# A graph network's edge stage: TensorE's and ScalarE's operations of one step in another order

## What is computed

```python
m_input  = concatenate([x[src], x[dst], edge_attr], axis=-1)   # 100000 x 320
h        = relu(m_input @ W1 + b1)                             # 100000 x 128
messages = relu(h @ W2 + b2)
agg      = segment_sum(messages, dst)                          # 3125 x 128
updated  = x + relu(agg @ Wn + bn)
```

## Time and profile before

| | |
|---|---|
| median of the runs | 1943.5 us |
| profiled execution, its own time | 1940.99 us |
| its span, first to last instruction | 1939.0 us |
| TensorE busy, share of the span | 1594.3 us, 82% |
| GpSimd busy | 767.6 us, 40% |
| VectorE busy | 731.2 us, 38% |
| ScalarE busy | 692.8 us, 36% |
| mean granted TensorE clock | 0.967 |

### The profile page before, as it was taken

The page is one execution under the profiler, slowest core; times in us unless marked ns, Lnnn a source line. Parts: engine busy times, 40 slices in busy tenths (PEclk is TensorE's granted clock), DMA queues, the critical chain, the costliest instruction groups (busy, mean ns, idle before and its releaser), DMA issues.

```text
span 1939.0 us, 35472 instructions
## 1 busy us (share of the span) xinstructions
PE 1594.3 (82%) x10363; PEld 1041.1 (54%) x10364; DVE 731.2 (38%) x2702; ACT 692.8 (36%) x1413; POOL 767.6 (40%) x805
## 2 busy tenths in 40 slices
PE   2777777998996888888888888888888884994995
PEld 1444445544555666666666666666666663442444
DVE  7998893112233222222222222222222225365004
ACT  4666663002002443444444444444444445301001
POOL 3000000000003777777777777777777761000000
PEclk9999997999997999999999999999999996997998
DMA  1000000001005333333333333333333321000001
GB/s 54 0 0 0 0 0 3 1 1 38 0 1 141 88 80 82 81 81 81 82 81 80 82 82 80 81 81 81 82 81 82 80 67 38 5 1 2 1 0 34
DMA packets 158346, 93.71 MB, mean 48 GB/s; under 512 B 120529, under 2 KB 143824, under 8 KB 158296
## 3 DMA queue, kind: packets, MB, share of 16 engines
q0 software_dynamic: 25088, 51.43, 10.2%
q1 hardware_dynamic: 133208, 41.60, 8.8%
HBM read 86.44 MB, written 6.52 MB: 48 GB/s over the span
## 4 chain that ended last, share of the span: by engine, by line
POOL 26%; PE 18%; issue 17%; DMA 3%; DVE 3%; ACT 1%; SPq 1%; POOLq 0%; DVEq 0%; ACTq 0%
POOL arena L607 26%; PE ps L726 8%; PE ps L929 3%; DMA arena<-x_w1a,idx 2%; PE ps L845 1%; PE ps L855 1%; PE ps L838 1%; PE ps L834 1%; DVE arena L1335 1%; PE ps L825 1%; DMA x_w1b<-arena 0%; DVE stats L1325 0%; PE ps L863 0%; PE ps L939 0%; PE ps L960 0%
## 5 line engine op out<-in xcount | busy, mean ns | idle before, releaser
L607 POOL DMA_INDIRECT arena<-x_w1a,idx x784 | 740.6, 945 | 832.2 <-issue 824.2
L726 PE MATMUL ps<-adj,arena 128*128 (+2 forms) x1875 | 367.7, 358 | 14.6 <-DVE arena L1300 7.9
L726 PEld LDWEIGHTS ps<-adj,arena 128*128 128x128 bf16 x1875 | 172.1, 99 | 203.2 <-issue 26.0
L1473 DVE TENSOR_TENSOR arena<-win_i,drel 128x96 f32<-128x96 f32 x196 | 50.7, 259 | 554.7 <-PE ps L855 551.3
L1117 ACT ACTIVATE arena<-arena 128x512 f32<-128x512 f32 x196 | 123.6, 631 | 302.6 <-DVE arena L1479 302.6
L834 PE MATMUL ps<-ident_f,arena 128*128 128x128 f32 x784 | 126.7, 284 | 126.1 <-DMA arena<-x_w1a,idx 126.1
L845 PE MATMUL ps<-w_c,arena 128*128 128x128 f32 x1568 | 226.9, 288 | 0.0
L660 PE MATMUL ps<-arena 128*128 128x300 bf16 x784 | 164.8, 296 | 63.1 <-DVE arena L1287 63.1
L1113 ACT ACTIVATE arena<-ps,cols 128x512 f32<-128x512 f32 x196 | 134.8, 688 | 218.2 <-PE ps L838 218.2
L845 PEld LDWEIGHTS ps<-w_c,arena 128*128 128x128 f32 x1568 | 189.7, 191 | 40.1 <-issue 40.1
L855 PE MATMUL ps<-arena 128*24 128x128 f32 x1568 | 206.6, 275 | 2.2 <-ACT arena L1117 2.2
(11 more groups left out here) (167 smaller groups left out, 1242.1 us busy)
## 6 DMA issues: line engine op xcount, KB each, us to landing
arena<-in_edge_attr SPq DMA_DIRECT2D x196, 128.0 KB, 2.2
arena<-x_w1a,idx POOLq DMA_INDIRECT x784
arena<-x_w1b SPq DMA_DIRECT2D x196, 12.0 KB
x_spill<-arena SPq DMA_DIRECT2D x1, 1600.0 KB, 7.7
x_w1a<-arena SPq DMA_DIRECT2D x6, 256.0 KB, 2.3
x_w1b<-arena SPq DMA_DIRECT2D x6, 256.0 KB, 2.4
arena<-x_spill SPq DMA_DIRECT2D x6, 256.0 KB, 4.6
out_x<-arena SPq DMA_DIRECT2D x3, 512.0 KB
```

The source lines that it names most:

```text
L607: pool.indirect_dma_start(out=z_e[v][:, j * D:(j + 1) * D], out_offset=None, in_=xa_d[:, :], in_offset=bass.IndirectOffsetOnAxis(ap=idx[:, ...
L726: last = pe.matmul(ps[:, u, 0:w], parts[q][:, k, :], adj[:, k, bass.ds(c0, w)], start=(k == 0 and q == 0), stop=(k == NT - 1 and q == 2))
```

## The change

TensorE's step had the order `hidden_t`, `inputs_t`, `sum_nodes`, `messages`, `window`; it gets `inputs_t`, `sum_nodes`, `hidden_t`, `window`, `messages`. ScalarE's step had `hidden_relu`, `inputs_out`, `take_sums`, `message_relu`; now `take_sums` stands first. The waits of each operation stay with it. Which block each works on stays too.

```diff
@@ TensorE
             def step(i, v, first=False, left=2):
 
 
-                if left >= 1:
-                    hidden_t(*at(i, v + 1))
                 if left >= 2:
                     inputs_t(*at(i, v + 2))
                 if not first:
                     sum_nodes(*at(i, v - 1))
-                messages(i, v)
+                if left >= 1:
+                    hidden_t(*at(i, v + 1))
                 if not first:
                     window(*at(i, v - 1))
+                messages(i, v)
@@ ScalarE
             def step(i, v, left=2, first=False):
+                if not first:
+                    take_sums(*at(i, v - 1))
                 if left >= 1:
                     hidden_relu(*at(i, v + 1))
                 if left >= 2:
                     inputs_out(*at(i, v + 2))
-                if not first:
-                    take_sums(*at(i, v - 1))
                 message_relu(i, v)
```

## The result

The changed kernel takes 2020.1 us, median of four runs (2014.4 to 2021.7), against 1943.1 us for the kernel before (four runs, one more than in the table above): a ratio of 1.039, 95% interval 1.037 to 1.041. The forecast was 2000.0 with a range of 1980 to 2026, slower. The profiled execution took 2021.46 us, 80.5 us more than that of before; its span is 2019.4 us, 80.4 us more.

A forecast was written before the change was run, and what follows sets the result against it. GpSimd's gathers (5.00 us a block) bound the kernel before; after, 632.6 + 194 x 5.27 + 4.34 put the last node sums at 1659.3, 56.5 us later, so 1943.5 + 56.5 = 2000.0 us, range 1980 to 2026.

The forecast's parts named there:

- The bound before: Edge stage before: GpSimd's gathers set the pace, 5.00 us a block, against 4.29 us of TensorE work.
- The chain: Messages (L845), VectorE's bias add, ScalarE's ReLU, node sums (L855): 2.60 us from start to start.
- pause: TensorE idle ahead of the node sums (L855) in each step after the change: 0.98 us.
- The ring: TensorE's step after, L845, L855, L834, L838, L863 and L845 again: 5.27 us, longer than the gathers' 5.00; 78 in 100.
- the seam from L838 to L863: First-layer matmuls to turned sums, never side by side before: unsure; each new seam at most 0.1 us more.
- The start: First step of the edge stage: first node sums at 632.6 us, against 632.29 before.
- The end: Last step, without L834 and L838: 4.34 us, last node sums starting at 1659.3 us.
- L855's wait: Node sums wait for ScalarE's ReLU in some 195 steps, about 1.0 us each, near 195 us.
- GpSimd's wait for the indices: GpSimd waits for VectorE's index copy (L1449), some 0.27 us a block, 50 us.
- the gathers stay the bound: Rival: TensorE's step under 5.00 us, TensorE still waits for gathers, 1943.5 us; 8 in 100.
- The loop's edge: Rival: VectorE's 1.04 us idle every four steps, counted as nothing, comes to stand outside: 2025 to 2050 us; 10 in 100.
- The clock: Rival: TensorE's pauses bring half clock in the edge stage; over one step in twenty 2043 us; 4 in 100.

The follow-up runs named there:

- e5: Kernel before, with two of a block's four gathers left out from the fifth block on (stale rows used): 1806.7 us, ratio 0.930.
- e6: Changed kernel, with two of a block's four gathers left out from the fifth block on: 2019.3 us, ratio 1.040 to the kernel before.
- e7: Changed kernel without VectorE's bias add of the messages; ScalarE's ReLU reads PSUM itself: 1940.2 us, ratio 0.9995 to the kernel before.
- e8: Changed kernel with the first-layer sum (L834, L838) ahead of the node sums again: 1946.0 us, ratio 1.0021 to the kernel before.
- e9: Changed kernel with the turned sums (L863) behind the messages again: 1940.7 us, ratio 0.9992 to the kernel before.
- e12: ScalarE's part of the change alone, TensorE in the old order: 1940.9 us, ratio 0.9995 to the kernel before.
- e10: Changed kernel with 88 rows in place of 24 for the turned sums (L863), added ones against zeros: 1960.0 us, ratio 1.0091 to the kernel before.
- e1: TensorE's part of the change alone, ScalarE in the old order, on the first chip: 2567.6 us, 1.120 of the kernel before there.

## Why the prediction was right, and which sizes were off

*The bound before.* Right: GpSimd's gathers, not TensorE with its 87%. Without half of them 1806.7 us, forecast 1809 before e5.

*The chain.* Right to 0.01 us: 2.61 us from L845 to L855, forecast 2.60 from the earlier trace rows. The forecast 0.98 us of pause shows as 0.90 in brackets, since L825's modelled end is 0.08 late.

*The ring.* Right as a mechanism (e6, e7, e8 and e9 each break or leave alone one of its parts), and too short by one term. Forecast 5.27, measured (1674.94 - 634.85) / 194 = 5.361 us. The term is L838's 0.86, read where L825 follows; ahead of L863 it is 0.96. The prediction counts it among the terms that "are read as they stand" (it speaks of seven, the sum has five), though the same paragraph names the seam from L838 to L863 as unsure and bounds it at 0.1 us. Over 194 steps the 0.091 us make 17.7 of the 21.6 us that were missing at the last node sums.

*The start.* Too short by 2.3 us, and the order isn't shown to be the cause. The sum has the first step at full clock and the first node sums at 632.6; they start at 634.85, with the clock at 0.50 from 628 to 632 us. In the kernel before it had risen by then:

```profile
628.00:632.00 4.00, 4.00 (x25) 2.80 (x24) 0.77 (x2) 2.41 (x6) 1.79 (x2) 0.97 0.47 115
```

TensorE's new wait of 0.83 us for the feature copy lies ahead of this stretch, but it doesn't settle when the clock rises. e6 has the same first steps with the same wait, and there the clock is up behind it:

```profile
629.18 0.61 PE L825 MATMUL ps<-ident_f,arena 128*88 128x128 f32 x4 [0.83 <-ACT arena L1108]
...
633.43 1.05 PE L855 MATMUL ps<-arena 128*24 128x128 f32 x8 [0.38 <-ACT arena L1117]
```

e5 and e12 have TensorE's old order without this wait, and their clock rises as late as in the changed kernel: from the stage's first transposition to the first node sums they take 12.97 and 12.82 us, the changed kernel 13.03, e6 10.34 and the kernel before 10.36. So with either order a profile can have this part or not.

*The end.* Also the clock. The last steps have less work, TensorE pauses for 1.44 us in place of 0.90 ahead of the node sums at 1669.58 and 1674.94, and the clock falls at about 1675 us. Rows of the last steps:

```profile
1670.56 0.66 PE L834 MATMUL ps<-ident_f,arena 128*128 128x128 f32 x4
...
1674.94 1.51 PE L855 MATMUL ps<-arena 128*24 128x128 f32 x8 [1.44 <-ACT arena L1117]
1676.81 0.62 PE L863 MATMUL ps<-ident_f,arena 24*128 24x24 f32 x2 [0.35 <-ACT arena L1122]
1677.35 2.08 PE L845 MATMUL ps<-w_c,arena 128*128 128x128 f32 x8
1680.88 1.90 PE L855 MATMUL ps<-arena 128*24 128x128 f32 x8 [1.45 <-ACT arena L1117]
```

5.94 us in the last ring in place of 4.34: 1.6 us. In e8, with the same pauses of 1.44 us in its last steps, the clock stays at 1.00 until they are over and the last ring is 4.34. Together 17.7 + 2.3 + 1.6 = 21.6, and the last node sums start at 1680.88 against 1659.3 forecast. What follows them took 2.3 us more than before in the profile, 2.0 of them in the first 20 us, in which TensorE is at half clock for longer; the sum had it "as before". The median moved 77.0, the profiled execution 80.5.

*The signs.* L855's wait came out as 176.0 us for some 195, since the brackets show 0.90 for the 0.98. GpSimd's wait for the indices came out as 99.5 us for 50: the longer ring gives it 0.36 us a block, 70 us, and 24 more stand in place of "issue" time (203.6 for 227.2 us).

*The rivals.* That the gathers stay the bound was to decide at 5.00 us, and e7, e9 and e10 bracket that point: rings of 4.60 and 4.84 us cost nothing, 5.06 us costs 18 us (15 of them in the steps), 5.36 us 77. The loop's edge cost nothing, as counted: VectorE's 49.9 us are there and no step in four is longer. The clock in the steady part stayed at 1.00 with a pause of 0.9 us in every step; the half clock cost 2.3 us at the start and 3.6 at the end instead, which the prediction had not priced.

## What to carry to other kernels

Where one engine's list holds both ends of a chain over other engines, add up what stands between the two ends and compare it with the chain: 2.21 us of work covered 1.51, 0.53 did not, and all that had stood between waits behind. Compare the resulting ring with the pace of what bounds now, here 5.36 with 5.00. Below that point the kernels tried here lost nothing or little (e7 and e9 nothing, e8 4.5 us); what is left shows in the steps that the bound doesn't cover, the last ones. A term read beside one neighbour holds for that neighbour: in new neighbourhoods the terms here moved by up to 0.10 us, up (L838 ahead of L863) and down (the chain behind L838 in e9), in every step.

## What the runs showed that was not expected

The weight load of the turned sums isn't started ahead. With 24 rows L863's load starts with its matmul (1103.71), with 88 rows the first one starts 0.43 us before (1102.68 for 1103.11), beside the long matmuls of L838; together that is 0.10 us before L863 and 0.18 behind it, per step. L825 and L845 (e9) behind L838 have the 0.86 us of the 88 rows. In e8, where L855 (24 columns) follows L838, the distance is 0.96 too (1101.49 to 1102.45), but what it waits for, ScalarE's L1117, ends only at 1101.80, so this doesn't show that few columns do the same. Why the load of 24 rows isn't ahead, the runs don't say; only 24 and 88 rows were tried.

The chip mattered more than the change. On the first chip the kernel before took 2293.9 us, on the other 1941.9 us. The four kernels profiled on the first show waits such as one of VectorE for the messages of 6.2 us (e1), and a TensorE clock of 0.73 to 0.88 between 700 and 1500 us. There e9's kernel was 1.1% faster than the kernel before (0.989, 0.985 to 0.994), and equal on the other. The cause of the gaps, and of that gain, stays open. No version that does all the gathers beats the kernel before on the other chip: e9, e12 and e7 meet it at 1940 to 1941 us, since all are held by the gathers.
